# First pass of a four-layer graph kernel: a tile's next rows turned 13 steps behind its end, split at 20, projected at 18, biased at 27

## The chip, the cores and the metric

One core of one Trainium2 chip. The metric is device microseconds of one execution of the whole program, the median of several runs.

## The reference

Four graph layers over 3125 nodes with 512 features, each added to its input. Cut to what matters here:

```python
h = relu(layernorm(x))
x = x + relu(segment_sum((h @ W0)[src] * edge_weight, dst))      # first layer: 53125 edges
h = relu(layernorm(x))
x = x + relu(segment_sum(norm * (h @ W1.T + b1)[row], col))      # second layer
# a third layer (two products, summed over neighbours) and a fourth (attention) follow
```

## The kernel before

The nodes are cut into 25 tiles of 125 rows. The edges lie in chunks of 128, and the first layer's sum over neighbours is a pass of 440 **steps** (`STEPS`). In a step, POOL gathers the 128 source rows of a chunk by an indirect DMA into one of 11 places of `ring` (L2295), DVE makes a 128x125 selection matrix `sel` (L1137, 12 places), and PE multiplies the two into the PSUM bank of the step's tile (L1879, two matmul records for one fp32 product). So POOL may run 11 steps ahead of PE's finished steps, and DVE 12: both wait on the semaphore `stepped`, which each step of PE raises. When a tile's steps are done, ACT copies its sums out (L1665, semaphore `kept`) and empties the bank.

Beside the steps, the second layer's dense part is made tile by tile, and this is what the change moves. Steps are counted from a tile's nominal end e (`ENDS`, 17 or 18 apart). A tile's sums may be complete up to 6 steps before e, since the tiles are sorted by size. On two engines, in the same order of steps:

- **DVE, e+12, `next_rows`**: adds the sums to x (L876), normalises (L894 to L908, 13 instructions) and raises `ln_h`. The result goes to one buffer, `h1_rows`.
- **PE, e+10, turning**: waits for `ln_h` and transposes the rows into PSUM by 4 matmuls (L1834), raises `pj_tr`.
- **DVE, e+18, `next_turned` (splitting)**: waits for `pj_tr`, writes the high part (L915) and the low part (L917), raises `pj_lo`.
- **PE, e+16, `project`**: waits for `pj_lo`, 12 matmuls with the second layer's weights (L1845), raises `pj_z`.
- **DVE, e+25, `next_made` (biasing)**: waits for `pj_z`, adds the bias and writes the projected rows (L1126). The halves of the rows are written a little later, at even steps (`z_halves`).

DVE and PE are in-order: what stands behind a waiting instruction waits too. The order is written out by hand in the two loops over i, DVE's at L1132 and after, PE's at L1948 and after. Up to step 321 the degrees of the nodes are counted beside the steps as well: DVE makes one-hot rows (L871), PE counts them (L1921). From step 200, DVE also makes tables for the next stage (L927, L930 and others).

After the pass, the next stage (`BSTEPS`, 590 steps of number j) counts edges by group: DVE makes two one-hot matrices (L1062 for five steps at once, L1064 for each), at most 10 steps ahead of PE (`HOTS`); PE multiplies them (L2010); ACT takes them out and empties the bank (L1701, L1705). Before it, PE waits for the last tile's sums and opens its banks (L1991, 8 matmul records). The last two tiles' next rows are made here: tile 23 (the last but one) is split before j = 0 and biased at j = 4; tile 24 is normalised at j = 12, turned at j = 16, projected at j = 36, biased at j = 46.

Of the kernel before, what the change touches and what calls it, by code (L numbers as in the profile page):

```python
# [26 lines left out]
def build(nc, x_in, src_in, dst_in, w_in, W0_in, W1_in, b1_in, G1_in, g1_in, G2_in, g2_in,  # L27
# [5 lines left out]
    TILES = N // TN  # L33
# [93 lines left out]
    ended = {end: k for k, end in enumerate(ENDS)}  # L127
# [14 lines left out]
    with ctx:  # L142
# [441 lines left out]
        def vector_program():  # L584
# [549 lines left out]
            for i in range(STEPS):  # L1134
                if i >= SELS:
                    V.wait_ge(stepped, step_value(i - SELS))
                V.tensor_scalar(out=sel[:, i % SELS, :], in0=node_iota[:, :], scalar1=dl_t[:, i:i + 1],  # L1137
                                scalar2=w_t[:, i:i + 1], op0=ALU.is_equal, op1=ALU.mult).then_inc(sel_ok, 1)
                if i == BEHIND - 1:
                    for k in range(KB):  # L1140
                        V.wait_ge(w_hi, KB + k + 1)
                        V.tensor_tensor(wl[:, k, :], bank[4 + k], wh[:, k, :].bitcast(F32), ALU.subtract).then_inc(w_lo, 1)
                if i >= BEHIND:
                    next(work, None)
                    next(work, None)
                if groups < SGROUPS and DEG_STEPS[groups] + 2 == i:
                    place_hots(groups)
                    groups += 1
                if i >= GROUPS_AT and i % 2 == 0 and i < KEYS_AT:
                    next(tables_work, None)  # L1150
                if i >= KEYS_AT:
                    next(keys_work, None)
                if (i - TURN_KEYS_AT) % 3 == 0 and 0 <= (i - TURN_KEYS_AT) // 3 < BRB:
                    take_keys((i - TURN_KEYS_AT) // 3)
                if i == SQUARES_AT + 7:
                    square_sum()
                if i == DEG_END:
                    root_of_degrees()
                k = ended.get(i - 12)
                if k is not None:  # L1160
                    next_rows(k)
                k = ended.get(i - 18)
                if k is not None:
                    next_turned(k)
                k = ended.get(i - 25)
                if k is not None:
                    next_made(k)
                    given += 1
                if i > DEG_END and i % 2 == 0 and scaled_rows < given:
                    z_halves(scaled_rows)  # L1170
                    scaled_rows += 1
# [659 lines left out]
        def tensor_program():  # L1831
# [119 lines left out]
            for i in range(STEPS):  # L1951
                step(0, i)
                if i == SQUARES_AT:
                    P.wait_ge(square_ok, 2)
                    P.wait_ge(pj_out, TILES)
                    P.matmul(bank[6][:, 0:1], ones[:, :], squares[:, 0:1], start=True, stop=True).then_inc(square_ok, 1)
                if i == SUM_AT:
                    P.wait_ge(group_counted, GROUPS - 1)
                    P.wait_ge(pj_out, TILES + SUM_TILE - 1)
                    P.matmul(bank[7][:, 0:GROUPS - 1], ones[0:EP, :], group_counts, start=True, stop=True).then_inc(below, 1)  # L1960
                if i == DEG_FROM:
                    P.wait_ge(w_lo, 2 * KB)
                    P.matmul(degrees_at(), zeros, wide[:, 0:TILES], start=True, stop=True)
                    P.wait_ge(deg_hot, TILES)
                if groups < SGROUPS and i == DEG_STEPS[groups]:
                    degree_group(groups)
                    groups += 1
                k = ended.get(i - 10)
                if k is not None:
                    P.wait_ge(ln_h, TILES + k + 1)  # L1970
                    P.wait_ge(w_lo, 2 * KB)
                    if k:
                        P.wait_ge(pj_lo, TILES + k)
                    turn_rows(TILES + k, h1_rows)
                k = ended.get(i - 16)
                if k is not None:
                    if k == 1:
                        P.wait_ge(square_ok, 4)
                    if k == SUM_TILE:
                        P.wait_ge(below, 3)  # L1980
                    if k >= 2:
                        P.wait_ge(pj_out, TILES + k - 1)
                    project(TILES + k)
                if (i - TURN_KEYS_AT + 8) % 3 == 0 and 0 <= (i - TURN_KEYS_AT + 8) // 3 < BRB:
                    turn_key_rows((i - TURN_KEYS_AT + 8) // 3)
# [6 lines left out]
            for j in range(BSTEPS):  # L1992
                if j % GROUP_STEPS == 0:
                    P.reg_load(tile_regs[0:GROUP_WORDS], group_words[0:1, j // GROUP_PACK:j // GROUP_PACK + GROUP_WORDS])
                if j == 16:
                    P.wait_ge(ln_h, 2 * TILES)
                    P.wait_ge(pj_lo, 2 * TILES - 1)
                    turn_rows(2 * TILES - 1, h1_rows)
# [617 lines left out]
```

## Time and profile before

| | us |
|---|---|
| median of 3 runs | 2884.88 (2884.67 to 2888.58) |
| the profiled execution's own time | 2887.89 |
| its span | 2886.6 |
| first pass, first gather to last | 110.4 to 783 |
| PE busy in the span | 2494.7 (86%) |
| DVE busy | 1818.6 (63%) |
| POOL busy | 877.3 (30%) |

The profile gives engine time by source line (a line can be a helper's), the idle time of an engine ahead of a group of instructions with what ended it, and the granted clock of TensorE. "remote" is a releaser that the profile could not name.

### The profile page before, as it was taken

What the parts mean: (1) busy time and instruction counts of PE and PEld (TensorE: products, weight loads), DVE (VectorE), ACT (ScalarE), POOL (GpSimd) and SP (SyncE); (2) the same over time, 40 slices, a digit from 0 to 9 for tenths busy, and PEclk for the clock granted to TensorE, in tenths of its full rate; (3) what the DMA queues carried; (4) which work ended last, traced back from release to release, by engine and by line L of the source; (5) the groups of instructions that cost most, each with busy time, mean ns of one, the idle gap of its engine ahead of it and who ended that gap; (6) DMA issues with size and microseconds to landing.
All of it is one profiled execution on the core that took longest, in us unless ns stands there. A gap on an engine that the chain in (4) does not pass through costs nothing.

```text
span 2886.6 us, 38664 instructions
## 1 busy us (share of the span) xinstructions
PE 2494.7 (86%) x9907; PEld 1388.4 (48%) x9907; DVE 1818.6 (63%) x4596; ACT 614.4 (21%) x1144; POOL 877.3 (30%) x900
## 2 busy tenths in 40 slices
PE   7888887778888888999899999998898788888877
PEld 5534444333432224666555565564688633333332
DVE  8665569577577775667333334344777687777666
ACT  4654420000056662000000000001565200000000
POOL 0466666666500000000000000000101466666665
PEclk9989999999977777999999999998999799999999
DMA  6686665566535444344611112111645367776665
GB/s 168 180 239 179 182 178 150 149 185 180 161 44 108 63 63 78 87 119 115 191 45 57 55 55 58 55 37 51 173 137 157 108 192 210 206 233 192 190 192 170
DMA packets 157069, 389.13 MB, mean 135 GB/s; under 512 B 44859, under 2 KB 46260, under 8 KB 156881
## 3 DMA queue, kind: packets, MB, share of 16 engines
q0 software_dynamic: 72400, 232.34, 28.0%
q1 hardware_dynamic: 83798, 153.04, 21.0%
q8 instruction: 114, 1.87, 0.3%
q10 hardware_dynamic: 683, 1.28, 0.2%
q14 instruction: 74, 0.61, 0.1%
HBM read 333.81 MB, written 52.72 MB: 134 GB/s over the span
## 4 chain that ended last, share of the span: by engine, by line
PE 58%; DVE 20%; issue 9%; DMA 7%; another core or an unknown queue 3%; POOL 2%; ACT 1%; SPq 0%; DVEq 0%; ACTq 0%
PE banks L1879 17%; PE banks L2016 16%; PE banks L2010 7%; PE banks L1845 6%; PE banks L2193 4%; DMA ring<-edge_counts 3%; DMA ring<-table,src_t 2%; DVE sel L1137 2%; POOL ring L2349 2%; DVE spare L1064 1%; PE banks L1834 1%; DVE spare L1062 1%; DVE ring L1616 1%; DVE rstd L901 1%
## 5 line engine op out<-in xcount | busy, mean ns | idle before, releaser
L1879 PE MATMUL banks<-ring,sel 128*125 128x512 f32 x1682 | 891.0, 657 | 156.3 <-issue 104.0
L1879 PEld LDWEIGHTS banks<-ring,sel 128*125 128x125 f32 x1682 | 287.4, 199 | 476.2 <-issue 472.9
L2295 POOL DMA_INDIRECT ring<-table,src_t x440 | 440.3, 1001 | 236.0 <-issue 104.0
L2327 POOL DMA_INDIRECT x<-table,src_t x25 | 24.0, 959 | 1445.0 <-ACT spare L1778 1439.2
L2349 POOL DMA_INDIRECT ring<-table,src_t x401 | 385.7, 962 | 217.9 <-issue 96.2
L2016 PE MATMUL banks<-acc,ring 125*125 125x512 f16 x1900 | 438.3, 381 | 8.1 <-DVE ring L1265 6.6
L1616 DVE TENSOR_TENSOR ring<-ring,banks 128x512 f32<-128x512 f32 x388 | 256.1, 682 | 126.6 <-DMA ring<-table,src_t 106.6
L2016 PEld LDWEIGHTS banks<-acc,ring 125*125 125x125 f16 x1900 | 257.2, 137 | 161.9 <-issue 28.9
L2010 PE MATMUL banks<-spare 128*125 128x450 f16 x590 | 265.3, 516 | 49.6 <-DVE spare L1064 25.0
L2010 PEld LDWEIGHTS banks<-spare 128*125 128x125 f16 x590 | 92.9, 158 | 221.7 <-issue 220.7
L2193 PE MATMUL banks<-bias_bc,spare 123*128 123x224 bf16 x1320 | 164.4, 270 | 14.6 <-issue 7.6
L1845 PE MATMUL banks<-wh,hTh 128*125 128x512 f32 x300 | 135.8, 453 | 47.3 <-DVE spare L1351 14.4
L1465 DVE TENSOR_REDUCE big<-banks 128x16 f32<-128x448 f32 x220 | 130.8, 617 | 54.0 <-PE banks L2193 45.2
L1064 DVE TENSOR_SCALAR spare<-node_scores,flags 128x450 f16<-128x450 f16 x590 | 155.9, 332 | 0.0
L1062 DVE TENSOR_TENSOR spare<-node_scores,den 128x625 f16<-128x625 f16 x118 | 95.6, 810 | 72.3 <-PE banks L2010 72.1
L2016 PE MATMUL banks<-acc,sel 125*125 125x512 f16 x600 | 140.6, 379 | 0.0
L1137 DVE TENSOR_SCALAR sel<-node_iota,dl_t,w_t 128x125 f32<-128x125 f32 x440 | 135.4, 352 | 8.1 <-remote 3.8
L1719 ACT ACTIVATE spare<-banks 125x512 f32<-125x512 f32 x25 | 14.9, 597 | 564.1 <-PE banks L2016 564.1
L2193 PEld LDWEIGHTS banks<-bias_bc,spare 123*128 123x128 bf16 x1320 | 119.8, 101 | 21.4 <-issue 12.9
L1665 ACT ACTIVATE acc<-banks 125x512 f32<-125x512 f32 x25 | 14.9, 597 | 518.6 <-PE banks L1879 286.3
L1845 PE MATMUL banks<-wl,hTh 128*125 128x512 f32 x300 | 123.9, 413 | 0.0
L1845 PE MATMUL banks<-wh,hTl 128*125 128x512 f32 x300 | 123.8, 413 | 0.0
(411 smaller groups left out, 3117.4 us busy)
## 6 DMA issues: line engine op xcount, KB each, us to landing
ring<-edge_counts SPq DMA_DIRECT2D x35, 683.6 KB
edge_counts<-big SPq DMA_DIRECT2D x175, 97.7 KB
ring<-table,src_t POOLq DMA_INDIRECT x841
sel<-edge_counts SPq DMA_DIRECT2D x11, 683.6 KB
acc<-dst_places SPq DMA_DIRECT2D x28, 256.0 KB
x<-dst_places SPq DMA_DIRECT2D x27, 256.0 KB
acc<-src_digits SPq DMA_DIRECT2D x28, 224.0 KB
x<-src_digits SPq DMA_DIRECT2D x27, 224.0 KB
```

The source lines that it names most:

```text
L1062: V.tensor_tensor(low_room[:, j % HOTS:j % HOTS + LB, :], low_names[:, None, :].to_broadcast([128, LB, TN]), low_t[:, j:j + LB, None].to_b ...
L1064: V.tensor_scalar(out=key_hot[j % HOTS], in0=key_names, scalar1=key_t[:, j:j + 1], scalar2=None, op0=ALU.is_equal).then_inc(hot_ok, 1)
L1137: V.tensor_scalar(out=sel[:, i % SELS, :], in0=node_iota[:, :], scalar1=dl_t[:, i:i + 1], scalar2=w_t[:, i:i + 1], op0=ALU.is_equal, op1=A ...
L1465: V.tensor_reduce(ue[:, pair_step(n):pair_step(n) + 2, :], bank[2 + n % 4][:, 0:2 * CTH].rearrange("p (i t h) -> p i h t", i=2, h=H), axis ...
L1616: V.tensor_tensor(slot, slot, weights[:, :, None].to_broadcast([CE, H, DP]), ALU.mult).then_inc(scaled, 1)
L1845: last = P.matmul(to, a[:, q, k, :], b[:, k, :], start=(k == 0 and n == 0), stop=(k == KB - 1 and n == 2))
L1879: last = P.matmul(to, sel[:, n % SELS, :], rows, start=False, stop=True, skip_group_check=True)
L2010: P.matmul(to, low_hot[j % HOTS], key_hot[j % HOTS], start=False, stop=True, skip_group_check=True).then_inc(built, 1)
L2016: last = P.matmul(to[0:TN, :], counts_at(n, s), acc16[0:TN, s, half * D:(half + 1) * D], start=(s == half == 0), stop=(s == TILES - 1 and ...
L2193: last = P.matmul(bank[2 + n % 4][:, i * CTH:(i + 1) * CTH], sp_hot[k % 3][0:SK, j * CE:(j + 1) * CE], u3[0:SK, part, :], start=(part == 0 ...
L2295: G.indirect_dma_start(out=ring[:, i % RING, :], out_offset=None, in_=table[0][:, :], in_offset=bass.IndirectOffsetOnAxis(ap=src_t[:, i:i ...
L2349: G.indirect_dma_start(out=rows_at(i), out_offset=None, in_=table[1][:, :], in_offset=bass.IndirectOffsetOnAxis(ap=src_t[:, i:i + 1], axis ...
```

## The change

The four distances are changed, and nothing else in the loops: turning e+10 to e+13, splitting e+18 to e+20, projecting e+16 to e+18, biasing e+25 to e+27. `next_rows` stays at e+12. Tile 23 ends at step 422, so its projection would fall on step 440, behind the last; it is given at j = 1 of the next stage.

```diff
@@ DVE, first pass
-                k = ended.get(i - 18)
+                k = ended.get(i - 20)
                 if k is not None:
                     next_turned(k)
-                k = ended.get(i - 25)
+                k = ended.get(i - 27)
                 if k is not None:
                     next_made(k)
@@ PE, first pass
-                k = ended.get(i - 10)
+                k = ended.get(i - 13)
                 if k is not None:
                     P.wait_ge(ln_h, TILES + k + 1)
...
-                k = ended.get(i - 16)
+                k = ended.get(i - 18)
@@ PE, next stage
+                if j == 1:
+                    P.wait_ge(pj_out, 2 * TILES - 3)
+                    project(2 * TILES - 2)
```

DVE's order between the biasing of tile 2 (L1126) and the next rows of tile 3 (L876), before. L1137 makes a step's selection matrix, L871 is the degree count's one-hot rows:

```order
L1126 TENSOR_TENSOR acc<-banks,bias_bc 125x512 [waits pj_z,w_in_sb]
L1137 TENSOR_SCALAR sel<-node_iota,dl_t,w_t 128x125 [waits stepped] x3
L871 TENSOR_TENSOR stage<-banks,stage 128x4x125 [waits deg_sum]
L1137 TENSOR_SCALAR sel<-node_iota,dl_t,w_t 128x125 [waits stepped] x2
L871 TENSOR_TENSOR stage<-banks,stage 128x4x125 [waits deg_sum]
L876 TENSOR_TENSOR x<-x,acc 125x512 [waits rows_loaded0,kept]
```

And now:

```order
L1126 TENSOR_TENSOR acc<-banks,bias_bc 125x512 [waits pj_z,w_in_sb]
L1137 TENSOR_SCALAR sel<-node_iota,dl_t,w_t 128x125 [waits stepped]
L871 TENSOR_TENSOR stage<-banks,stage 128x4x125 [waits deg_sum]
L1137 TENSOR_SCALAR sel<-node_iota,dl_t,w_t 128x125 [waits stepped] x2
L871 TENSOR_TENSOR stage<-banks,stage 128x4x125 [waits deg_sum]
L876 TENSOR_TENSOR x<-x,acc 125x512 [waits rows_loaded0,kept]
```

Three selection matrices stand between the two in place of five: the biasing moved two steps, the next rows did not.

PE's order at the end of the pass, before: from the last two of the twelve matmuls of tile 23's projection to the opening of the next stage's banks.

```order
L1845 MATMUL banks<-wl,hTh 125x512
L1845 MATMUL banks<-wh,hTl 125x512
L1875 REGISTER_ALU [waits sel_ok,got10]
L1875 REGISTER_ALU
L1879 ISA [waits fresh]
L1879 MATMUL banks<-ring,sel 125x512
L1991 MATMUL banks<-b_bc,ident 125x450 [waits keys_ok,kept]
L1991 MATMUL banks<-b_bc,ident 125x450 x3
```

And now (the change's lines are 3 further on from there):

```order
L1879 MATMUL banks<-ring,sel 125x512
L1991 MATMUL banks<-b_bc,ident 125x450 [waits keys_ok,kept]
L1991 MATMUL banks<-b_bc,ident 125x450 x3
L1994 TENSOR_LOAD stage
L2011 REGISTER_ALU [waits low_ok,hot_ok]
L2013 REGISTER_ALU [waits room]
L2013 ISA
L2013 MATMUL banks<-spare 125x450
L1845 MATMUL banks<-wh,hTh 125x512 [waits pj_lo,pj_out]
```

The projection of tile 23 went from ahead of the pass's last step to behind the next stage's first product.

## Rows read from the trace of the kernel before

**Rows 1.** The page: busy time by engine, granted clock in 40 slices.
```profile
PE 2494.7 (86%) x9907; PEld 1388.4 (48%) x9907; DVE 1818.6 (63%) x4596; ACT 614.4 (21%) x1144; POOL 877.3 (30%) x900
PEclk9989999999977777999999999998999799999999
```
**Rows 2.** Stretches: window, length, busy PE, PEld, DVE, ACT, POOL, clock, DMA share, GB/s.
```profile
207.00:389.00 182.00, 159.50 (x582) 81.90 (x581) 105.07 (x294) 82.58 (x224) 119.11 (x125) 0.97 0.63 179
418.70:502.70 84.00, 63.06 (x213) 32.30 (x213) 81.03 (x173) 3.59 (x6) 53.75 (x51) 0.90 0.55 156
```
**Rows 3.** Groups by line from 150 to 850 us: busy, mean ns | idle before.
```profile
L2295 POOL DMA_INDIRECT ring<-table,src_t x412 | 410.7, 997 | 206.3 <-issue 96.7 <-PE banks L1879 87.3 <-remote 22.3
L1845 PE MATMUL banks<-wh,hTh 128*125 128x512 f32 x100 | 49.0, 490 | 12.3 <-DVE hTl L917 10.0 <-issue 2.2
L1834 PE MATMUL banks<-ident,stage 125*128 125x125 f32 x100 | 17.9, 308 | 38.3 <-DVE stage L908 21.7 <-issue 16.6
L1126 DVE TENSOR_TENSOR acc<-banks,bias_bc 125x512 f32<-125x512 f32 x25 | 17.2, 689 | 117.0 <-remote 88.2 <-PE banks L1845 21.7 <-issue 6.9
L915 DVE TENSOR_SCALAR hTh<-banks 128x500 fp32r<-128x500 f32 x25 | 17.1, 683 | 47.8 <-remote 40.2 <-PE banks L1834 4.1 <-issue 3.6
```
**Rows 4.** Timeline around tile 3's turning and splitting: start, length, what.
```profile
237.12 0.65 PE L1834 MATMUL banks<-ident,stage 125*128 125x125 f32 x4 [0.94 <-issue]
...
239.49 0.33 DVE L1137 TENSOR_SCALAR sel<-node_iota,dl_t,w_t 128x125 f32<-128x125 f32 x1
...
243.90 0.94 POOL L2295 DMA_INDIRECT ring<-table,src_t  x1 [2.02 <-PE banks L1879]
245.31 0.68 DVE L915 TENSOR_SCALAR hTh<-banks 128x500 fp32r<-128x500 f32 x1 [5.49 <-remote]
246.03 0.68 DVE L917 SCALAR_TENSOR_TENSOR hTl<-banks,hTh 128x500 fp32r<-128x500 f32 x1
...
246.85 0.46 PE L1845 MATMUL banks<-wh,hTh 128*125 128x512 f32 x1 [1.49 <-DVE hTl L917]
```
**Rows 5.** The same view around tile 13's turning.
```profile
510.61 0.59 PE L1834 MATMUL banks<-ident,stage 125*128 125x125 f32 x4
...
511.24 0.68 DVE L915 TENSOR_SCALAR hTh<-banks 128x500 fp32r<-128x500 f32 x1 [1.13 <-PE banks L1834]
```
**Rows 6.** The same view from tile 3's biasing to tile 4's turning.
```profile
257.03 0.69 DVE L1126 TENSOR_TENSOR acc<-banks,bias_bc 125x512 f32<-125x512 f32 x1 [6.78 <-remote]
...
260.08 0.68 DVE L876 TENSOR_TENSOR x<-x,acc 125x512 f32<-125x512 f32 x1
...
264.83 0.65 PE L1834 MATMUL banks<-ident,stage 125*128 125x125 f32 x4 [2.13 <-issue]
```
**Rows 7.** Stretches by clock: behind tile 4's turning, and tile 7's projection.
```profile
266.00:270.00 4.00, 3.96 (x10) 1.38 (x9) 1.47 (x5) 0.00 (x0) 1.98 (x2) 0.63 0.75 207
352.00:357.60 5.60, 5.47 (x13) 4.30 (x14) 3.56 (x10) 5.60 (x17) 4.26 (x5) 0.50 0.64 184
```
**Rows 8.** Waits from 418 to 502 us: waiter <- releaser: total, times, longest.
```profile
PE banks L1834 <- DVE stage L908: 9.6, 2, 5.4
```
**Rows 9.** Chain of waits, 339 to 362 us: start, length, what.
```profile
345.12 5.46 another core or an unknown queue
350.60 0.68 DVE hTh L915
...
352.13 5.45 PE banks L1845 x12
```
**Rows 10.** Timeline from 784 to 807 us, the seam of pass and next stage.
```profile
792.66 0.69 DVE L1126 TENSOR_TENSOR acc<-banks,bias_bc 125x512 f32<-125x512 f32 x1 [4.05 <-PE banks L1845]
...
798.92 0.81 DVE L1062 TENSOR_TENSOR spare<-node_scores,den 128x625 f16<-128x625 f16 x1 [3.62 <-PE banks L2010]
...
800.39 0.68 DVE L876 TENSOR_TENSOR x<-x,acc 125x512 f32<-125x512 f32 x1
...
805.79 1.71 PE L2010 MATMUL banks<-spare 128*125 128x450 f16 x3 [3.40 <-DVE spare L1064]
```

## The prediction

> **What bounds the kernel now.** The page first: PE is busy for 86% of the span [rows 1]. The change touches the first pass alone, about 110 to 783 us, and the seam behind it, so the rest is left as it is. In the pass I read the stretches, then the idle time by line, then the timeline of single tiles.
>
> The stretches show two different regimes [rows 2]. From 418.7 to 502.7 us DVE is busy for 81.03 of 84 us: DVE is the bound there, because the tables for the next stage are made beside the steps. From 207 to 389 us (seven tiles, 26.0 us each) nobody is full: PE 159.5 of 182, DVE 105.1, POOL 119.1. There the engines wait for each other in a ring. POOL needs finished steps to reuse a place, PE needs gathered rows and DVE's matrices, DVE needs PE's turning and projection.
>
> The idle time by line names the waits of that ring [rows 3]. PE stands 38.3 us ahead of turning, for the normalised rows. It stands 12.3 us ahead of projecting, for the split. DVE stands 47.8 us ahead of splitting and 117.0 us ahead of biasing, most of it ended by a releaser the profile can't name. POOL's 412 gathers are busy 410.7 us and idle for 206.3, of which some 0.3 us each is its own issue and over 80 us is waiting for PE's steps.
>
> Tile 3 shows how one round goes [rows 4]. The turning starts at 237.12 us and lasts 0.65. DVE has made its last matrix ahead of the split by 239.82 us, two microseconds after the turning is done, and yet it starts splitting at 245.31. By then PE has done the six steps that stand between turning and projecting and has nothing left but the projection, which starts at 246.85 after 1.49 us of standing still. In tile 13, where DVE was already waiting, the split starts at 511.24, as soon as the turning ends at 511.20 [rows 5]. So a signal of PE is sometimes seen at once and sometimes some 7.5 us late, and I can't say from the trace why. The chain of waits runs through this very place in tile 7: 5.46 us of an unknown queue, the split, the projection [rows 9].
>
> **The change part by part.** No work is added or removed: the same 100 turning matmuls, 300 of projection, 25 splits and 25 biasings. What moves are places in two in-order queues. POOL's, ACT's and SP's orders stay. Three terms:
>
> *1. Turning at e+13.* On paper PE gets three steps more before it needs the rows. It doesn't get all of them: DVE makes the matrix of step e+13 only behind the normalising, so PE runs steps 11 and 12 and then stands at step 13 for the same normalising as before. What really gets shorter is DVE's road from biasing one tile to normalising the next. It takes from 257.03 to 260.08 us now for tile 4 [rows 6], and two matrices fall out of it, at 0.33 us each [rows 4], so 0.7 us. PE's own distance stays: both the biasing and the place where it stands are two steps later. Of the 38.3 us, 9.6 in two waits lie where DVE is the bound [rows 8, 2]; shortening those buys nothing, since DVE's work is the same. That leaves 28.7 us, in about 13 tiles. 13 x 0.7 = **9 us less**. The ends are 0 (PE only waits for gathered rows instead) and 28.7 (all of it goes).
>
> *2. Projecting at e+18.* Between turning and projecting stand five steps now, not six. Where the signal of turning comes promptly that costs nothing. Where it comes late, PE reaches the projection one step earlier and stands there one step longer. The profile names such late splits with 40.2 us in all, the longest near 5.5, so about ten tiles. A step in that stretch takes at most (245.36 - 237.77)/6 = 1.27 us with the counting beside it (245.36 is where PE's 1.49 us of standing begins) [rows 4]. I take 0.9, since part of the 1.27 is waiting itself: 10 x 0.9 = **9 us more**. The ends are 0 and 12.7.
>
> *3. The seam.* PE's total work up to j = 1 is unchanged, so its second product still starts at about 797.8 us. But tile 23's projection ends there instead of before 792.66, and DVE, in order, biases it about 5.2 us later. DVE's own idle time ahead of L1062 was 3.62 us and is eaten up by that [rows 10]; the remaining 1.6 us shift tile 24's rows from 800.39 to 802.0 and PE's halt of 3.40 us at 805.79 to about 5.0. **1.6 us more**, with 0 (caught up later) and 5.2 as ends. The next stage's PE is nearly full, so I don't count on the catching up.
>
> The biasing itself is not behind anything new: it stays nine steps behind the projection, and `z_halves` follows it where DVE has room or, in the full stretch, costs what it did.
>
> Sum: -9 + 9 + 1.6 = +1.6 us. The profiled execution took 2887.89 us, 3.0 above the median of 2884.88, so the sum is 2889.5 against the profiled time and **2886.5** against the median; I give the latter.
>
> On the size of term 2 a rule speaks against me. The trace shows a prompt signal in tile 13 and a late one in tile 3. The Trainium skill, page "Perfetto Trace Analysis", section "Tensor Engine Instruction (MATMUL, LD_WEIGHTS)", says that TensorE's profiled end is an estimate and that the signal goes out once PSUM has acknowledged the last bytes. By that alone every split would follow its turning as in tile 13, term 2 would be 0 and the sum 2877.5. Tile 3's 5.49 us of idle DVE are against it, and the measurement decides.
>
> **The rivals.**
>
> *Faster: PE's halts really go.* If a late signal comes because PE itself stands still at the projection and not after a fixed time, one step less between them costs nothing, and the shorter round lets POOL refill sooner. For it: POOL's wait of 2.02 us ends 1.4 us before DVE's [rows 4], as if one event had freed both. The clock also speaks for it. Behind tile 4's halt of 2.13 us [rows 6] the granted clock is 0.63 for 4 us, and tile 7's projection runs at 0.50, the 1.2 GHz level, for 5.45 us [rows 7, 9]; fewer halts may save such falls, at up to 2.7 us each. Against it: DVE still makes e+13's matrix behind the normalising. Term 1 then lies between 9 and 28.7, say 19: 2884.9 - 19 + 1.6 = 2867.5.
>
> *Slower: PE stands longer at the projection.* The place is L1845 at e+18. If the turning's signal takes longer than PE needs for five steps, PE halts there in each of ten tiles for a whole step more, and the clock may fall behind it as in tile 7. Term 1 comes to nothing, since PE's extra steps only eat up gathered rows earlier. Then 2884.9 + 12.7 + 1.6 = 2899, and 2.7 us more for each further fall of the clock, 2907 with three. It decides as soon as term 2 exceeds term 1 by 4.2 us.
>
> *Nothing moves.* PE's halt only changes its line, from L1834 to L1879 waiting for `sel`, and POOL's gathers set the pace. At (410.7 + 96.7)/412 = 1.23 us for a gather and its issue [rows 3] they need 21.7 us for 17.6 steps against 26.0 a tile now, so they are near but not the bound. Then only the seam remains: 2886.5, the same number as my sum by another road.
>
> **How the numbers follow.** A measurement of this kernel tells a change from none at about 0.2%, 5.8 us. Forecast and "nothing moves" together: 0.38. Faster rival: 0.36, since no term of the loss is as well seen as PE's 38.3 us. Slower rival: 0.20, and 0.06 for a seam or a full stretch that goes worse than term 3 says. The likeliest case alone would reach from 2880.7 to 2890.7. The range takes in both rivals up to their first numbers, 2862 to 2900: below it lies the case in which nearly all 28.7 us go, above it the one with several falls of the clock.
>
> **What would show each step.** Term 1: idle time ahead of L1834 falls from 38.3 to near nothing, and idle time ahead of L1879 "<-DVE sel L1137" rises to take part of it; DVE's idle time ahead of L1126 changes little. Term 2: idle time ahead of L1845 rises from 12.3 to about 20. Term 3: L1126 of tile 23 starts some 5 us later against the first L2010, and the halt of PE near j = 13 grows from 3.4 to about 5 us. The prediction is wrong if L1845's idle time doesn't rise (the faster rival) or if the pass from 207 to 389 us takes more than 183 us with L1845's halts above 20 us (the slower one). If the pass is unchanged and the total is not, the seam was mis-sized.

## The result, and the profile after

| | before | changed |
|---|---|---|
| median of 17 runs, us | 2887.25 | 2891.80 |
| lowest to highest | 2882.22 to 2896.10 | 2885.47 to 2904.50 |
| profiled execution: own time, span | 2887.89, 2886.6 | 2892.98, 2891.7 |

The changed kernel takes 1.0021 times as long, with a 95% interval from 1.0012 to 1.0031. That is +6.1 us, 3.5 to 9.0. The forecast was +1.6 us, with a likeliest case of 2880.7 to 2890.7; 2891.8 us lies just above that and inside the range of 2862 to 2900. In part that is because the kernel before itself now has a median of 2887.25 us and not 2884.88.

Two lines of the page of the changed kernel, busy time and granted clock:

```profile
PE 2491.3 (86%) x9907; PEld 1391.4 (48%) x9907; DVE 1818.9 (63%) x4596; ACT 614.6 (21%) x1144; POOL 874.5 (30%) x900
PEclk9899999888978778999999999998999799999999
```

Both lines read nearly as before [rows 1], as the work is the same. The two stretches, with the columns of [rows 2]:

```profile
207.00:389.00 182.00, 160.26 (x575) 85.14 (x574) 104.61 (x294) 80.61 (x220) 119.83 (x125) 0.93 0.63 178
418.70:502.70 84.00, 64.00 (x214) 32.33 (x213) 81.17 (x172) 3.59 (x6) 54.64 (x51) 0.90 0.56 158
```

The quiet stretch now goes from tile 2's next rows at 207.39 us to tile 9's at 389.33, 181.9 us against 182.0. Seven tiles with the new distances take as long as with the old ones. (In the kernel before, L876 starts at 207.02 us for tile 2 and at 389.06 for tile 9.) Now the groups by line from 150 to 850 us, busy time, mean ns, and idle time ahead with what ended it:

```profile
L1834 PE MATMUL banks<-ident,stage 125*128 125x125 f32 x100 | 18.0, 311 | 0.0
L1845 PE MATMUL banks<-wh,hTh 128*125 128x512 f32 x100 | 51.2, 512 | 23.2 <-DVE hTl L917 17.1 <-issue 6.1
L1879 PE MATMUL banks<-ring,sel 128*125 128x512 f32 x845 | 427.9, 635 | 63.6 <-issue 35.5 <-DMA ring<-table,src_t 14.9 <-DVE sel L1137 11.9
L1921 PE MATMUL banks<-big,stage 128*125 128x25 bf16 x440 | 41.5, 220 | 20.5 <-DVE stage L871 12.5 <-issue 8.0
L915 DVE TENSOR_SCALAR hTh<-banks 128x500 fp32r<-128x500 f32 x25 | 16.9, 675 | 84.6 <-remote 78.0 <-issue 5.8 <-PE banks L1834 0.8
L1126 DVE TENSOR_TENSOR acc<-banks,bias_bc 125x512 f32<-125x512 f32 x25 | 17.2, 690 | 104.1 <-remote 76.8 <-PE banks L1845 21.5 <-issue 5.7
```

The same view of the kernel before has two PE groups that did not stand among [rows 3]:

```profile
L1879 PE MATMUL banks<-ring,sel 128*125 128x512 f32 x841 | 432.7, 644 | 51.4 <-issue 31.2 <-DMA ring<-table,src_t 17.4 <-DVE sel L1137 1.6
L1921 PE MATMUL banks<-big,stage 128*125 128x25 bf16 x440 | 41.9, 219 | 4.4 <-issue 2.7 <-DVE stage L871 1.5
```

PE's 38.3 us ahead of the turning [rows 3] are gone to the last tenth. But PE stands 12.2 us longer ahead of the steps (L1879, where "<-DVE sel L1137" rises from 1.6 to 11.9 as foretold), 16.1 longer ahead of the counting of degrees (L1921) and 10.9 longer ahead of the projection. Before, the four groups add up to 38.3 + 12.3 + 51.4 + 4.4 = 106.4 us; after, to 0.0 + 23.2 + 63.6 + 20.5 = 107.3. The standing time changed its place and kept its size. This sum is no second piece of evidence beside the time of the pass: where the work stays and the pass takes as long, what is left over has to be the same. What it adds is where the time went.

The second place is the seam. The timeline of the changed kernel, from the last steps of the pass to tile 24's rows (start, length, what, idle time ahead):

```profile
786.90 3.60 PE L1879 MATMUL banks<-ring,sel 128*125 128x512 f32 x8
789.19 1.32 DVE L1064 TENSOR_SCALAR spare<-node_scores,flags 128x450 f16<-128x450 f16 x5
790.54 0.60 ACT L1665 ACTIVATE acc<-banks 125x512 f32<-125x512 f32 x1 [21.95 <-PE banks L1879]
791.19 4.91 PE L1991 MATMUL banks<-b_bc,ident 1*125 1x450 f32 x8 [0.69 <-ACT acc L1665]
796.03 0.64 PE L2013 MATMUL banks<-spare 128*125 128x450 f16 x1
796.16 0.94 PE L1845 MATMUL banks<-wh,hTh 128*125 128x512 f32 x1
...
800.65 0.93 PE L2013 MATMUL banks<-spare 128*125 128x450 f16 x4
800.92 0.69 DVE L1126 TENSOR_TENSOR acc<-banks,bias_bc 125x512 f32<-125x512 f32 x1 [10.41 <-PE banks L1845]
804.94 0.68 DVE L876 TENSOR_TENSOR x<-x,acc 125x512 f32<-125x512 f32 x1
...
810.32 1.74 PE L2013 MATMUL banks<-spare 128*125 128x450 f16 x3 [3.56 <-DVE spare L1064]
```

PE finishes the steps at 790.5, waits 0.69 us for the last kept tile, clears its banks with eight products of one row (L1991), makes one comparison and then projects tile 23 until 800.8. VectorE has made its five rows of comparisons by 790.5 and stands 10.41 us at the biasing, where it stood 4.05 before, and ends 8.3 us later [rows 10]. Tile 24's next rows start 4.6 us later than before [rows 10]. The next stage's comparisons on PE, by the view of their line (shortest, median, longest ns, first and last start), before and after:

```profile
L2010 PE MATMUL banks<-spare x590: 351/582/632, 797.3 to 1116.6; 128*125 128x450 f16 x197
```
```profile
L2013 PE MATMUL banks<-spare x590: 351/400/637, 796.0 to 1119.9; 128*125 128x450 f16 x197
```

They take 323.9 us instead of 319.3. The added 4.6 us are as much as the projection that now lies among them takes, 4.65 us. VectorE's last selection of the pass starts at 784.6 us, 2.2 later than the 782.4 of before; from there to the last comparison it is 335.3 us against 334.2.

VectorE's last selection is a poor start for that count, since PE uses it only later: PE ends the last step 11.0 us behind it before, tile 23's projection included, and 5.9 us behind it now. Counted from PE's end of the last step (793.41 and 790.50 us) to the last comparison it is 323.2 us before, with tile 23 already projected, and 329.4 now, with its projection still to come. Less the 3.36 us that the projection took in the pass, that is 326.0, so the seam is 2.8 us longer. In the same way the pass without tile 23's projection ends 0.5 us later than before, and the rest behind the last comparison takes 1.8 us more. That makes up the 5.1 us between the two profiled spans.

### The profile page after: what moved, and what is told of

The parts are those of the page before. It is cut to its first block, busy times and chain, and to the rows that moved or that the text cites. A ratio compares the mean times of both kernels' runs of the same rounds, so it can differ in the third digit from the quotient of the medians.

```text
span 2891.7 us, 38666 instructions
## 1 busy us (share of the span) xinstructions
PE 2491.3 (86%) x9907; PEld 1391.4 (48%) x9907; DVE 1818.9 (63%) x4596; ACT 614.6 (21%) x1144; POOL 874.5 (30%) x900
## 4 chain that ended last, share of the span: by engine, by line
PE 52%; DVE 23%; issue 8%; DMA 7%; another core or an unknown queue 5%; POOL 3%; ACT 1%; SPq 0%; DVEq 0%; ACTq 0%
PE banks L2019 16%; PE banks L1879 12%; PE banks L2013 7%; PE banks L1845 6%; PE banks L2196 4%; POOL ring L2352 3%; DVE sel L1137 3%; DMA ring<-edge_counts 3%; DMA ring<-table,src_t 3%; DVE spare L1064 2%; DVE stage L871 1%; DVE spare L1062 1%; PE banks L1834 1%; DVE ring L1616 1%
## 5 line engine op out<-in xcount | busy, mean ns | idle before, releaser
L1879 PE MATMUL banks<-ring,sel 128*125 128x512 f32 x1682 | 883.3, 653 | 170.3 <-issue 105.9
L1879 PEld LDWEIGHTS banks<-ring,sel 128*125 128x125 f32 x1682 | 285.7, 198 | 480.1 <-issue 476.9
L2013 PE MATMUL banks<-spare 128*125 128x450 f16 x590 | 262.6, 505 | 54.2 <-DVE spare L1064 26.5
L1845 PE MATMUL banks<-wh,hTh 128*125 128x512 f32 x300 | 138.5, 462 | 57.6 <-DVE hTl L917 17.1
L1137 DVE TENSOR_SCALAR sel<-node_iota,dl_t,w_t 128x125 f32<-128x125 f32 x440 | 136.0, 355 | 9.2 <-PE banks L1879 8.0
L1062 DVE TENSOR_TENSOR spare<-node_scores,den 128x625 f16<-128x625 f16 x118 | 95.5, 810 | 67.2 <-PE banks L2013 66.7
L1845 PE MATMUL banks<-wl,hTh 128*125 128x512 f32 x300 | 127.6, 425 | 0.0
L1845 PE MATMUL banks<-wh,hTl 128*125 128x512 f32 x300 | 127.0, 423 | 0.0
L1701 ACT CAST big<-banks 125x450 f16<-125x450 f32 (+1 forms) x175 | 96.1, 549 | 135.3 <-PE banks L2013 134.4
```

What stands on the lines that cost most here:

```text
L1062: V.tensor_tensor(low_room[:, j % HOTS:j % HOTS + LB, :], low_names[:, None, :].to_broadcast([128, LB, TN]), low_t[:, j:j + LB, None].to_b ...
L1845: last = P.matmul(to, a[:, q, k, :], b[:, k, :], start=(k == 0 and n == 0), stop=(k == KB - 1 and n == 2))
L1879: last = P.matmul(to, sel[:, n % SELS, :], rows, start=False, stop=True, skip_group_check=True)
L2013: P.matmul(to, low_hot[j % HOTS], key_hot[j % HOTS], start=False, stop=True, skip_group_check=True).then_inc(built, 1)
```

## The experiments

Twelve runs of ten kernels were made, in three sets of four, each set beside the kernel before on one chip. The sets differ: the kernel before took 2731.20 us in the first, 2902.28 in the second and 2900.04 in the third. The record numbers the chips 0, 10 and 0 and does not say whether the two with number 0 are the same one, so I speak of sets. Only ratios within one set are compared, and the kernel before has a profile only from the main measurement. In the table a version is given by its distances behind a tile's end (turning / split / projection / biasing) and by the place of tile 23's projection: "pass" is where the kernel before has it, "stop" directly behind the last step, ahead of the wait for the kept tile, and "stage" behind the first comparison, as in the change.

| run | distances | tile 23 | against before, % (95%) | set |
|---|---|---|---|---|
| e1_seam_only | 10/18/16/25 | stage | +0.27 (+0.08 to +0.45) | 1 |
| e2_no_seam | 13/20/18/27 | stop | -0.11 (-0.23 to 0.00) | 1 |
| e3_turn13_only | 13/18/16/25 | pass | -0.02 (-0.16 to +0.12) | 1 |
| e4_turn10 | 10/20/18/27 | stage | +0.11 (-0.02 to +0.25) | 1 |
| a_change | 13/20/18/27 | stage | +0.16 (-0.01 to +0.33) | 2 |
| e5_bias_at_9 | 13/20/18/27 | stage | +0.21 (+0.03 to +0.40) | 2 |
| e6_in_the_hole | 13/20/18/27 | stop | 0.00 (-0.16 to +0.16) | 2 |
| e7_turn10_no_seam | 10/20/18/27 | stop | +0.35 (+0.21 to +0.50) | 2 |
| e8_hole_only | 10/18/16/25 | stop | -0.04 (-0.15 to +0.07) | 3 |
| e9_turn13_again | 13/18/16/25 | pass | +0.20 (+0.07 to +0.33) | 3 |
| e10_seam_again | 10/18/16/25 | stage | +0.15 (0.00 to +0.30) | 3 |
| e11_turn13_hole | 13/18/16/25 | stop | +0.26 (+0.11 to +0.42) | 3 |

### Parts of the change, first set

**The seam alone.** On PE, in the kernel before:

```
-                if k is not None:
+                if k is not None and k < TILES - 2:
...
+                if j == 1:
+                    P.wait_ge(pj_out, 2 * TILES - 3)
+                    project(2 * TILES - 2)
```

> The kernel before, with tile 23's projection alone moved from two steps before the end of the first pass to behind the first comparison of the next stage. Theory A (the extra time is made of the seam and of the projection standing nearer to its turning): in the changed kernel next rows of tile 24 are 2.4 us later against tile 23's than before, and the biasing of tile 23 waits 10.4 us in place of 4.1; so this kernel alone is +2.4 us (0 to +5), some 2889.7, with the next stage's first PE work little moved and the biasing of tile 23 as late as in the change. Theory B (the later turning costs) and theory C (the later biasing costs): the seam hides under the idle of the next stage, +0 us (-1.5 to +1.5).

Measured: 2739.45 us against 2731.20, +0.27%, +7 us with an interval from 2 to 12. VectorE stands 14.21 us at the biasing of tile 23. The seam by itself costs as much as the whole change. Theories B and C, which gave it nothing, miss here; what they say of the later turning and of the later biasing comes back in other sets (e9, e7). The profiled execution, 2724.27 us, was the shortest of its ten, so its profile need not show what costs.

**The change without the seam.**

```
-                k = ended.get(i - 18)
+                k = ended.get(i - 18) if i < STEPS - 1 else TILES - 2
...
-                if j == 1:
-                    P.wait_ge(pj_out, 2 * TILES - 3)
-                    project(2 * TILES - 2)
```

> The changed kernel, except that tile 23 is projected at the last step of the pass, so that nothing is left for the next stage. Theory A: the seam's 2.4 us are gone and the loss within the pass stays, so +2 to +4.5 us against the kernel before, some 2890.5; PE's idle time ahead of the projection still 20 to 25 us. Theories B and C: all of the loss stays, +5 to +7.

Measured: 2726.62 us, -0.11%, with the upper end at no change. This is below what every theory gave. Theory A's other half, a price for the nearer projection, doesn't show in this set: PE's idle time ahead of the projection is 2.3 us, not 20 to 25.

**The turning alone.**

```
-                k = ended.get(i - 10)
+                k = ended.get(i - 13)
```

> The kernel before, with the turning alone moved to 13 steps behind the tile's end; the split stays at 18 on VectorE, the projection at 16, three steps behind the turning in place of six, the biasing at 25. Theory A: PE's idle time ahead of the projection, 12.3 us with six steps and 23.2 with five, goes to 40 us or more, and the time to +6 to +14 us. Theory B: what the later turning costs is the same as in the change, +3 to +6, whatever the distance. Theory C: the biasing is where it was, so within 1 us of the kernel before.

Measured: -0.02%, and 2.2 us idle ahead of the projection where theory A said 40 or more. Theory A misses by the whole amount, theory C is met here, but not in the third set (below).

**The change with the turning back at 10.** The same line, from 13 to 10.

> The changed kernel with the turning back at 10 steps: split 20, projection 18 (eight steps behind the turning), biasing 27, seam as changed. Theory A: PE's idle time ahead of the projection falls under 8 us, that ahead of the turning is back at some 38 us, and what is left is the seam, +2.4 us less a gain at the projection: -3 to +3 us. Theory B: the same sign, since the turning is back, -1 to +1 without a seam's price. Theory C: the later biasing is all there, so +5 to +7.

Measured: +0.11%, +3 us. Its idle time ahead of the turning is 14.2 us, not 38. With e1 to e3 it suggests one reading: the two versions with tile 23 in the stage have the longer times, the two without it do not. For e4 alone the interval includes no change.

### The seam, second set

**The change itself.**

> The changed kernel itself, beside the runs that follow. Theory S (formed on the first four runs: the seam costs some 7 us, since VectorE stands 10 to 16 us at the biasing of tile 23 with only five comparisons made ahead, and the moves within the pass give some 3 us): +3 to +5 us against the kernel before, and 0.3 to 0.4% above the version with tile 23 projected at the last step, if the chip is like that of the first four. Rival N (the seam's figure is noise of one set of runs): this kernel, the one with the biasing later and the one with the projection in the hole lie within 1.5 us of each other.

Measured: 2904.75 us against 2902.28, +0.16%. It agrees with the +0.21% of the first measurement and can't be told from it. By itself its interval just reaches no change.

**VectorE biases tile 23 later**, so that ten rows of comparisons are ready when it halts.

```
-                if j == 4:
+                if j == 9:
                     next_made(TILES - 2)
```

> The changed kernel with VectorE's biasing of tile 23 behind its tenth comparison row in place of its fifth, so that ten rows stand ready when it waits for the projection. Theory S: the wait at the biasing falls from 10 to 16 us to some 8 to 12, PE has ten comparisons in stock instead of five, and 2 to 3 us come back: +1 to +2 us against the kernel before. A rival within S (the loss is PE's: 3 us of projection moved behind PE's stop at the end of the pass): nothing comes back, since PE's stop and its projection stand as they were. Rival N: 0 against the change.

Measured: +0.21%. VectorE's wait fell as meant, from 10.35 to 6.75 us, and no gain shows. The rival that puts the loss on PE is nearer, but the two intervals leave room for the 2 to 3 us of theory S, and from the last selection to the last comparison this profile has 333.3 us against 335.0 in a_change. From PE's end of the last step, with 3.36 us taken off for the projection, it is 323.4 against 325.7, so the single profile speaks for theory S by 2.3 us. The timed runs don't show it, and this one is inconclusive.

**Tile 23 projected ahead of the wait for the kept tile.**

```
+            P.wait_ge(pj_out, 2 * TILES - 3)
+            project(2 * TILES - 2)
             P.wait_ge(kept, TILES)
...
-                if j == 1:
-                    P.wait_ge(pj_out, 2 * TILES - 3)
-                    project(2 * TILES - 2)
```

> The changed kernel with tile 23's projection on PE right behind the pass's last step, ahead of PE's wait for the last kept tile, during which it stood 4 to 6 us in every profile. Theory S: VectorE's wait at the biasing is back at 3 to 5 us, the projection's 3 us lie in PE's stop, and the whole seam's price comes back and up to 1 us more: -3 to -5 us against the kernel before, like the version with tile 23 projected at the last step. Rival N: 0 against the change.

Measured: 0.00%. It lies 0.16% below the change in the same set, which the two intervals alone don't prove. The expectation also described the place wrongly: in the change PE does not stand 4 to 6 us there, it waits 0.69 us and clears banks for the rest. The timeline of this kernel:

```profile
800.00 1.32 DVE L1064 TENSOR_SCALAR spare<-node_scores,flags 128x450 f16<-128x450 f16 x5
800.75 0.79 PE L1845 MATMUL banks<-wh,hTh 128*125 128x512 f32 x1
...
803.71 0.40 PE L1845 MATMUL banks<-wh,hTl 128*125 128x512 f32 x1
804.22 0.69 DVE L1126 TENSOR_TENSOR acc<-banks,bias_bc 125x512 f32<-125x512 f32 x1 [2.89 <-PE banks L1845]
...
807.25 2.94 PE L2012 MATMUL banks<-spare 128*125 128x450 f16 x10
```

The 0.69 us of the wait lie under the projection, and it runs at full clock: 3.36 us, where the change needs 4.65. The windows of the projection alone (L1845 on PE: window, length, busy, clock) in the kernel before, the change and this one:

```profile
788.90:793.40 4.50, 3.36 (x12) 1.00 0.00 0
```
```profile
795.90:801.00 5.10, 4.65 (x12) 0.64 0.00 0
```
```profile
800.60:805.00 4.40, 3.36 (x12) 1.00 0.00 0
```

It is so in every profile. In the eight with tile 23 in the pass or the stop its twelve products take 3.34 to 3.36 us at a clock of 1.00, the 2.4 GHz level. In the six with it in the stage they take 4.40 to 5.63 us at 0.57 to 0.73, partly at 1.2 GHz. Just ahead there PE works on the eight one-row products of L1991. In the change the clock is 1.00 from 784 to 790.5 us, 0.70 from 790.5 to 796 and 0.64 from 796 to 800.9. PE's windows of the change (window, length, its matmuls' busy time, clock, DMA share, GB/s):

```profile
784.00:790.50 6.50, 6.50 (x19) 1.00 0.25 79
...
790.50:796.00 5.50, 4.81 (x9) 0.70 0.00 0
796.00:800.90 4.90, 4.90 (x16) 0.64 0.00 0
```

The fall itself is not the change's. In all fourteen profiles the clock, which was 1.00 through the last steps, falls to 0.50 within 1.5 to 8.3 us of the start of the first one-row product. Where tile 23 is projected earlier the fall meets other work. In the kernel before it meets the first comparisons, and in e9, with tile 23 in the pass, the clearing of the banks, which takes 4.53 us there (PE's windows of the kernel before, then the line of e9):

```profile
797.30:798.00 0.70, 0.70 (x5) 1.00 0.00 0
798.00:801.40 3.40, 3.40 (x9) 0.50 0.00 0
```
```profile
805.28 4.53 PE L1991 MATMUL banks<-b_bc,ident 1*125 1x450 f32 x8 [0.69 <-ACT acc L1665]
```

So a slower projection is seen wherever tile 23 is in the stage, but a slower clearing isn't tied to it: it takes 3.28 us in e1 and e5, which have tile 23 in the stage, and 4.61 in e3, which has not.

**Split, projection and biasing later, turning at 10, no seam.** The edits of the turning at 10 and of the change without the seam together.

> The changed kernel with the turning back at 10 and tile 23 projected at the last step: only split, projection and biasing stand two steps later than in the kernel before. Theory S with the gain at the projection: PE's idle time ahead of the projection under 8 us (eight steps behind the turning), that ahead of the turning some 38; turning at 13 was worth nothing alone on the first chip, so this gives all of the -3 us of the moves within the pass, -2 to -5 us. Rival (the gain within the pass is the turning's, and the projection's distance costs nothing): 0 against the kernel before.

Measured: 2909.67 us, +0.35%, +10 us. Both theories miss, to the slow side. PE's standing is as expected (4.4 us ahead of the projection, 43.8 ahead of the turning), and the profiled execution, with a span of 2897.4 us, was the shortest of its runs, so its profile doesn't show what costs.

### What each part costs alone, third set

**The stop alone**, and with the turning at 13. The edit of e6 in the kernel before; then also the turning's line.

> The kernel before, with only tile 23's projection moved: from step 438 to behind the last step, into PE's stop ahead of the next stage. Theory P (from the profiles so far, measured from VectorE's last selection to the last comparison: 335.3 us in the kernel before, 334 to 336 with the projection behind the first comparison, 330 to 331 with it in the stop, on the chips of the long times; 340, 340 to 341 and 337 on the other): -3 to -5 us. Rival N (the place of this projection is worth nothing): 0, +-1.5 us.

> Turning at 13 with split 18, projection 16 and biasing 25 as before, and tile 23's projection in PE's stop behind the last step: the version that may beat both. Theory P: the sum of the two parts, -3 to -5 us on a chip of the short times, -8 to -16 us on one of the long times. Theory D: -5 to +2 us.

Measured: -0.04% and +0.26%. Moving tile 23's projection from the pass to the stop is worth nothing that can be told: rival N. The version meant to beat both kernels is slower than the kernel before: it measured +7.5 us, 15 above the nearer end of theory P, and theory D's end of +2 us is passed too.

**The turning alone and the seam alone, once more.**

> The kernel before with the turning alone at 13, once more. On a chip of the short times (some 2730 us) the same as on the first, -0.02% (0 +-3 us). On a chip of the long times (2885 to 2905): theory P holds that the later turning takes away PE's 38 us of stops ahead of it, which there cost time: -5 to -12 us, with PE's idle time ahead of the projection over 20 us. Theory D (the projection's nearness to its turning, three steps here against five in the change, gives the gain back): -2 to +6 us.

> The seam alone, once more (the first time +0.27%, with an interval from 0.08 to 0.45%). Theory S (the seam costs what the whole change costs): +4 to +8 us. Theory P (against the place before the end of the pass it costs only 0 to 1 us, since from last selection to last comparison the profiles differ by no more; it costs 4 to 5 us only against the stop): -1 to +2 us.

Measured: +0.20% (+5.8 us) for the turning alone, at the upper end of theory D, with 24.3 us idle ahead of the projection. Together with e11, two kernels have the projection three steps behind the turning in this set, and both are slower. The seam alone gives +0.15%, +4.4 us with an interval from 0 to 9: theory S, the low end of it. The two runs of the seam alone, weighted by the inverse squares of their intervals, give +0.20 +-0.12%, some +5.7 us on 2890 (2.3 to 9.1). The change without it (e2, e6) gives -0.07 +-0.09% in the same way.

One rival runs beside all of these sums. The same kernel, the turning alone, gave -0.02% (-0.16 to +0.12) in one set and +0.20% (+0.07 to +0.33) in another. Either the sets differ in what this change costs, or a kernel's figure scatters from set to set by more than its interval says. Only the change and the seam alone were measured twice besides, and these pairs agree. The rival isn't tested for the others: e7 and e11 stand on one run each.

The idle time of PE ahead of its four groups in the pass, from the groups by line between 150 and 850 us, in each profile:

| kernel | turning L1834 | projection L1845 | steps L1879 | degrees L1921 | sum |
|---|---|---|---|---|---|
| before | 38.3 | 12.3 | 51.4 | 4.4 | 106.4 |
| e8 | 28.0 | 21.0 | 51.2 | 6.8 | 107.0 |
| e10 | 33.7 | 13.8 | 56.3 | 8.0 | 111.8 |
| e7 | 43.8 | 4.4 | 52.9 | 2.8 | 103.9 |
| change | 0.0 | 23.2 | 63.6 | 20.5 | 107.3 |
| a_change | 0.0 | 9.9 | 73.5 | 26.5 | 109.9 |
| e5 | 0.0 | 17.4 | 66.0 | 25.1 | 108.5 |
| e6 | 0.0 | 11.6 | 72.4 | 24.3 | 108.3 |
| e9 | 0.0 | 24.3 | 64.6 | 21.5 | 110.4 |
| e11 | 0.0 | 28.7 | 60.6 | 21.6 | 110.9 |
| e1 (set 1) | 18.6 | 4.0 | 37.7 | 2.3 | 62.6 |
| e4 (set 1) | 14.2 | 5.0 | 37.9 | 2.7 | 59.8 |
| e2 (set 1) | 0.0 | 2.3 | 48.0 | 10.5 | 60.8 |
| e3 (set 1) | 0.0 | 2.2 | 46.9 | 13.1 | 62.2 |

Wherever the turning stands at 10, PE halts ahead of it; wherever it stands at 13, PE never does, and the degrees and the steps take it up. The sum stays within 8 us in the sets of the long times and within 3 in the other, as it has to where the work is the same and the pass takes about as long. The row of the steps in e9 shows who is waited for, which in the kernel before had been 1.6 us of `sel`:

```profile
L1879 PE MATMUL banks<-ring,sel 128*125 128x512 f32 x848 | 439.1, 647 | 64.6 <-issue 40.8 <-DMA ring<-table,src_t 15.7 <-DVE sel L1137 6.5
L1921 PE MATMUL banks<-big,stage 128*125 128x25 bf16 x440 | 41.9, 220 | 21.5 <-DVE stage L871 12.9 <-issue 8.4
```

## Why the prediction was right, and where its sizes were not

**Term 1, turning at 13: -9 us.** The signature came out: 38.3 to 0.0 ahead of L1834, the wait for `sel` up, while VectorE's idle time ahead of L1126, said to change little, fell from 117.0 to 104.1. The step "two matrices fall out of VectorE's road, so 0.7 us in each of 13 tiles" is not borne out as a gain. The road did get shorter: from the biasing of one tile to the next rows of the next VectorE took a median of 3.58 us before and 2.25 in the change. That comes from the later biasing, though, and not from the later turning: with the turning alone it is 3.05 us (e9). And a shorter road does little for PE: in e7 it is 2.25 us with the turning at 10, and PE stands 43.8 us ahead of the turning, not less than 38.3; in the first set e4 has 14.2 where e1, with the longer road, has 18.6. The later turning alone (e3, e9) gives -0.02 and +0.20%. The table shows what became of the vanished halt: PE stands instead for a degree's one-hot rows (from 1.5 to 12.5 us) and for a selection (from 1.6 to 11.9), the next things that VectorE owes it. That this is why nothing was gained is argued, not shown.

**Term 2, projecting one step nearer: +9 us.** The sign is supported, the size is not. In the sets of the long times the idle time ahead of L1845 is 4.4 us at eight steps of distance, 12.3 to 21.0 at six, 9.9 to 23.2 at five and 24.3 to 28.7 at three. So my sign for it, "12.3 to about 20", seemed met by the change's 23.2, but the same kernel showed 9.9 in its second profile: one profile can't tell one step here. At 9 us a step the turning alone would cost 3 x 9 - 9 = 18 us; e9 measured 5.8 (2 to 10).

**Terms 1 and 2 together: 0.** This holds: -0.07 +-0.09%, and 181.9 us in the quiet stretch. But they aren't two terms that add up. In the third and the second set the turning alone costs 5.8 us and split, projection and biasing alone (e7, with the stop, which is worth nothing) 10; together they cost nothing measurable. Taken at their word, these say that the places have to move with each other. Each half stands on sets in which a figure may scatter by as much, and which wait would make it slow I can't name.

**Term 3, the seam: +1.6 us, ends 0 and 5.2.** Right place, right sign, the size too small: +5.7 us (2.3 to 9.1), as much as the change's +6.1. The step that was mis-sized is "PE's total work up to j = 1 is unchanged, so its second product still starts at about 797.8 us": it starts at 800.65. I priced the moved work at the duration that it had in the pass. In the change the projection takes 4.65 us instead of 3.36, and in the other stage kernels 4.40 to 5.63, so 1.0 to 2.3 us are not in my term. The clearing of the banks ahead of it also takes longer, 4.91 us instead of 3.28, but it does so in kernels with tile 23 in the pass too, and the kernel before pays for the lower clock at its comparisons, so that part can't be put down to the change. If they add up, my 1.6 and the 1.0 to 2.3 make 2.6 to 3.9 us, inside the measured interval and near the 2.8 us between the two profiles. The rest of that step went roughly as put: the biasing was to come 5.2 us later and came 8.3, VectorE's wait of 3.62 us ahead of L1062 is gone, and PE's halt near j = 13, forecast to grow from 3.40 to about 5.0, is 3.56.

What stays open is the rest of the size. From PE's end of the last step to the last comparison, with 3.36 us taken off where the projection comes behind that end, the profiles of the long-time sets and of the main measurement give 323.2 us (before) and 322.7 (e9) with tile 23 in the pass, 319.7 to 321.9 with it in the stop, and 325.4, 326.0, 325.7 and 323.4 (e5) with it in the stage. So the stage costs some 2.8 us against the pass by these, while the timed runs give 5.7 with 2.3 as the lower end. The first set's profiles don't show it at all: 324.9 for e3 against 324.2 and 324.7 for e1 and e4, of which e1's is the shortest execution of its kernel. By the same count the stop lies 1 to 3 us below the pass, and its timed runs show no such gain, so single profiles are good to some 3 us here. Either the true value is at the low end of the interval, or they hide a part of it. And how it divides between PE's added time and VectorE's halt, e5 doesn't settle.

The likeliest case, 2880.7 to 2890.7, was also put together from two middles: 5.8 us below the forecast and 5.8 above the median of the kernel before. Around the forecast it would have reached to 2892.3 and taken in the measurement.

**The rivals.** "Nothing moves" is what happened in the pass: PE's halt changed its line, L1834 to L1879 and L1921. The faster rival wanted an idle time ahead of L1845 that doesn't rise; a_change has 9.9 us, below the 12.3 of the kernel before in the main measurement, and isn't faster, so the sign was a bad one. The slower rival wanted the quiet stretch above 183 us and got 181.9. The last sentence of the prediction was the one to keep: the pass is unchanged and the total is not, so the seam was mis-sized. That the total came out near the forecast owes something to luck, as terms 1 and 2 were each off and cancelled.

The rule quoted from the Trainium skill, page "Perfetto Trace Analysis", section "Tensor Engine Instruction (MATMUL, LD_WEIGHTS)", would have made term 2 nothing and the change 7 us faster than the kernel before. The rule gives no length for the acknowledgement, so a late signal contradicts my reading of it and not the page. In the long-time sets and the main measurement the trace is against that reading: in the change VectorE stands 84.6 us ahead of the split, 78.0 of them ended by a releaser that has no name. In the first set the trace agrees with it (last section).

No version beats both kernels. The best, tile 23's projection in the stop alone or with the whole change, can't be told from the kernel before (-0.11, 0.00, -0.04%).

## What to carry to other kernels

Before counting an engine's idle time ahead of a line as a gain, ask which of its other lines waits for the same engine, and after the change add the idle time up over all of them: here the halt moved to the next such lines, and the sum stayed. When a shift by a few steps pushes an item over the end of a loop, price that item by itself, at the clock of its new place and not at the duration it had in the loop; measured alone, the item here cost about as much as the whole change. And judge moves of single steps by repeated runs, as one profile gave 23.2 and another of the same kernel 9.9 us for the wait in question.

## What was not expected of the hardware

**The late signals come with the set of runs, not with the kernel.** The kernel with the turning alone at 13 ran in two sets, at a median of 2729.44 and of 2908.51 us. Its groups by line from 150 to 850 us, in the first:

```profile
L2295 POOL DMA_INDIRECT ring<-table,src_t x414 | 416.4, 1006 | 137.3 <-issue 91.7 <-PE banks L1879 45.6
L1126 DVE TENSOR_TENSOR acc<-banks,bias_bc 125x512 f32<-125x512 f32 x25 | 17.3, 691 | 31.4 <-PE banks L1845 31.2
L915 DVE TENSOR_SCALAR hTh<-banks 128x500 fp32r<-128x500 f32 x25 | 16.9, 676 | 88.3 <-PE banks L1834 81.5 <-issue 6.8
```

and in the third:

```profile
L2295 POOL DMA_INDIRECT ring<-table,src_t x416 | 412.2, 991 | 218.7 <-issue 97.9 <-PE banks L1879 91.3 <-remote 29.5
L1126 DVE TENSOR_TENSOR acc<-banks,bias_bc 125x512 f32<-125x512 f32 x25 | 17.3, 691 | 88.0 <-remote 69.4 <-PE banks L1845 18.0 <-issue 0.4
L915 DVE TENSOR_SCALAR hTh<-banks 128x500 fp32r<-128x500 f32 x25 | 16.9, 677 | 102.8 <-remote 86.9 <-PE banks L1834 8.3 <-issue 7.4
```

In the first set no wait of VectorE's at these lines ends with a releaser that has no name, and nearly all end with PE's own record; in the other 86.9 + 69.4 us end with such a "remote" releaser. A gather costs POOL the same (1006 and 991 ns), an operation on VectorE too. By first and last start of single lines, nearly all of the difference of some 180 us lies in the two stages with indirect gathers: 600.6 against 682.4 us from the first to the last selection (L1137), and 543.0 against 627.2 from the last L2193 to the last step (L1879). All between takes 1466.3 and 1484.5. PE's standing ahead of its four groups is 44% less in the first set (62.2 against 110.4 us), so the ring of waits that I reasoned about is another one there. The granted clock differs as well: from 207 to 389 us it is 1.00 in the first of the two profiles and 0.95 in the other. Whether the late signals and the lower clock are two effects or one I can't say, nor whether they belong to the chip or to something else that differed between the sets: no kernel was run twice on what is known to be one chip.

**The clock behind one-row products.** Being busy did not keep the clock here. The clearest case is e8, where PE goes from the projection straight into the eight one-row products and from them into the comparisons (window, length, PE busy, clock, DMA share, GB/s):

```profile
795.70:799.00 3.30, 3.30 (x14) 1.00 0.00 0
799.00:802.20 3.20, 3.20 (x9) 1.00 0.00 0
802.20:805.00 2.80, 2.80 (x10) 0.60 0.00 0
```

PE is busy for all of the 9.3 us, and the clock still falls behind the one-row products. That it is their single row of input that does it is a guess: no run put full products in their place, and in e6 the clock fell only 8.3 us after the first of them.
